# GNN weights in a PSUM bank, and the mix's softmax by eight biased, summing exponents

## The reference

```python
# GNN, one head: softmax over the edges that end in a node, times the rows of their sources
m = segment_max(e_h, dst); ex = exp(e_h - m[dst]); den = segment_sum(ex, dst)
out = segment_sum((ex / den[dst])[:, None] * z_h[src], dst)
# mix: softmax of q over the 32 features of each head
q = softmax(q, axis=-1) * SCALE
out = einsum('bhde,bhnd->bhne', context, q)
```

## Time and profile before

| | us |
|---|---|
| median of 3 runs | 2942.56 |
| lowest, highest | 2938.81, 2943.4 |
| the profiled execution | 2940.0 |
| its span, first to last instruction | 2937.9 |

### The profile page before, as it was taken

How to read it: one execution, slowest core, us unless ns; L and a number is a source line. 1 busy time by engine, 2 the same in 40 slices (tenths; PEclk the granted TensorE clock), 3 DMA queues, 4 the chain that set the end, 5 groups by cost and what they waited for, 6 DMA issues and landing times. The chain is left out here.

```text
span 2937.9 us, 21979 instructions
## 1 busy us (share of the span) xinstructions
PE 1496.6 (51%) x5476; PEld 949.3 (32%) x5476; DVE 2121.8 (72%) x3413; ACT 1206.4 (41%) x2381; POOL 2013.1 (69%) x1978
## 2 busy tenths in 40 slices
PE   2657730222212222222125179999899999984323
PEld 1433330111111111111025046555555555551122
DVE  6978889998888888888568255565655555657657
ACT  1532338776667776666334022222222232221012
POOL 0456457777777777777666677777777777777560
PEclk8878875555555555555555589999999999997666
DMA  4522547666666666666563312222222222222186
GB/s 137 186 68 68 148 126 238 229 225 214 209 204 216 219 218 207 218 218 213 190 176 105 107 30 49 49 67 51 49 49 49 49 53 53 61 50 44 17 304 230
DMA packets 222462, 395.96 MB, mean 135 GB/s; under 512 B 50867, under 2 KB 174370, under 8 KB 214912
## 3 DMA queue, kind: packets, MB, share of 16 engines
q1 hardware_dynamic: 137604, 263.49, 26.2%
q0 software_dynamic: 75632, 122.58, 18.0%
q10 hardware_dynamic: 9100, 8.50, 0.9%
HBM read 204.85 MB, written 189.59 MB: 134 GB/s over the span
## 5 line engine op out<-in xcount | busy, mean ns | idle before, releaser
L1234 POOL DMA_INDIRECT stage_got<-ffn_rows,setup_src_ffn x860 | 844.2, 982 | 261.8 <-issue 261.7
L1234 POOL DMA_INDIRECT edges_got<-gnn_rows,edges_src_gnn x728 | 756.4, 1039 | 241.7 <-issue 221.5
L1341 DVE TENSOR_TENSOR_SCAN stage_y<-stage_decays,stage_y 128x960 f32<-128x960 f32 (+2 forms) x256 | 520.7, 2088 | 5.1 <-issue 5.0
L2174 PE MATMUL stage_ph<-ffn_xt_all,stage_w 128*128 128x448 f32 x896 | 381.5, 566 | 102.0 <-ACT stage_hid L2235 40.3
L1357 ACT ACTIVATE stage_rows<-stage_y 128x3640 f32<-128x3640 f32 (+1 forms) x88 | 399.8, 4543 | 0.0
L1630 PE MATMUL stage_pm<-setup_ident,stage_mix_parts 128*128 128x128 f32 x98 | 33.4, 444 | 674.6 <-DVE stage_mix_parts L1703 602.3
L2296 DVE TENSOR_TENSOR stage_start_parts<-stage_pk,stage_of_tile 128x490 f32<-128x490 f32 x328 | 209.2, 667 | 115.8 <-PE stage_pk L2166 111.1
L2166 PE MATMUL stage_pk<-stage_start_parts 128*128 128x490 bf16 x984 | 244.3, 386 | 66.9 <-DVE stage_start_parts L2296 51.9
L1317 DVE TENSOR_TENSOR stage_y<-edges_got,stage_y 128x896 f32<-128x896 f32 x168 | 262.9, 1672 | 0.3 <-ACT stage_y L1299 0.3
L2174 PEld LDWEIGHTS stage_ph<-ffn_xt_all,stage_w 128*128 128x128 f32 x896 | 173.8, 197 | 243.9 <-issue 141.9
L1630 PEld LDWEIGHTS stage_pm<-setup_ident,stage_mix_parts 128*128 128x128 f32 x98 | 14.2, 204 | 705.0 <-DVE stage_mix_parts L1703 677.3
(11 more groups left out here) (481 smaller groups left out, 2903.3 us busy)
## 6 DMA issues: line engine op xcount, KB each, us to landing
state_gnn<-stage_rows SPq DMA_DIRECT2D x56, 1848.0 KB
y<-search_found SPq DMA_DIRECT2D x28, 896.0 KB, 4.2
tail_fin_y<-y SPq DMA_DIRECT2D x7, 3584.0 KB, 17.7
stage_got<-ffn_rows,setup_src_ffn POOLq DMA_INDIRECT x860
edges_got<-gnn_rows,edges_src_gnn POOLq DMA_INDIRECT x784, 3.6
state_ffn<-stage_rows SPq DMA_DIRECT2D x32, 384.0 KB, 2.4
mix_rows<-stage_mix_parts SPq DMA_DIRECT2D x49, 131.0 KB, 2.1
x_again_mix<-mix_rows SPq DMA_DIRECT2D x7, 917.0 KB, 6.1
```

Of the source, the lines that this page charges most:

```text
L1234: pool.indirect_dma_start(out=got[:, u, t, :], out_offset=None, in_=self.row_dram[g.name][:, :], in_offset=bass.IndirectOffsetOnAxis(ap=sr ...
L1341: ins = dve.tensor_tensor_scan(some, r[s][:, 0:b - a, :].rearrange("p c t -> p (c t)"), some, 0.0, ALU.mult, ALU.add)
L2174: mm = pe.matmul(ph[:, f % 2 * 2 + half, 0:HALF], w1[:, e, k, f * P:(f + 1) * P], xt_all[:, k, at(b * (B * P) + half * HALF, HALF)], start ...
```

## The change

The weights of the GNN get a PSUM bank of their own. ScalarE writes them there first (VectorE waits for that one), and a second time into `y`, where the scan and its own weighing want them; VectorE's three products read them from PSUM. In the mix the maximum is taken negated and kept for two tiles; ScalarE no longer exponentiates a shifted copy at once but reads `pq` directly, head by head, with that maximum as the bias, and accumulates each head's sum. Subtraction and sum on VectorE go; the maximum, the reciprocal and the product move to other places of the chunk; PE's next projection waits for the exponents.

```diff
+            weights = self.ps(stack, "weights", [P, 512])[:, 0:2 * H * T].rearrange("p (s h t) -> p s h t", s=2, h=H)
...
-                act.activation(y[:, s, C:C + H, 1:T + 1], pm[:, :, :], ACT.Exp).then_inc(w_ready, 1)
+                if g is GNN:
+                    act.activation(weights[:, s, :, :], pm[:, :, :], ACT.Exp).then_inc(w_ready, 1)
+                    act.activation(y[:, s, C:C + H, 1:T + 1], pm[:, :, :], ACT.Exp)
+                else:
+                    act.activation(y[:, s, C:C + H, 1:T + 1], pm[:, :, :], ACT.Exp).then_inc(w_ready, 1)
...
-                                            w[:, h, 0:n].unsqueeze(2).unsqueeze(3).to_broadcast([P, n, Q, KQ]), ALU.mult)
+                                            weights[:, s, h, 0:n].unsqueeze(2).unsqueeze(3).to_broadcast([P, n, Q, KQ]), ALU.mult)
...
-                        pe.wait_ge(q_shifted, t)
+                        pe.wait_ge(q_exp, t)
...
-                        act.wait_ge(q_shifted, t + 1)
-                        act.activation(q[:, 1 - s, :], q[:, 1 - s, :], ACT.Exp).then_inc(q_exp, 1)
+                        act.wait_ge(max_ready, t + 1)
+                        if t >= 2:
+                            act.wait_ge(q_turned, t - 1)
+                        for h in range(MIX_HEADS):
+                            d = at(h * MIX_DIM, MIX_DIM)
+                            ins = act.activation(q[:, 1 - s, d], pq[:, d], ACT.Exp, bias=mx[:, 1 - s, h:h + 1], scale=1.0,
+                                                 accum_out=sm[:, 1 - s, h:h + 1])
+                        ins.then_inc(q_exp, 1)
...
+                def q_max(t, s):
                     dve.wait_ge(projected, t + 1)
-                    dve.tensor_reduce(mx[:, :], by_head(pq[:, 0:D]), AX, ALU.max)
-
-                def q_shift(t, s):
-                    if not (isinstance(t, int) and t < 2):
-                        dve.wait_ge(q_turned, t - 1)
-                    dve.tensor_tensor(by_head(q[:, s, :]), by_head(pq[:, 0:D]), each(mx[:, :]), ALU.subtract).then_inc(q_shifted, 1)
-
-                def q_sum(t, s):
-                    dve.wait_ge(q_exp, t + 1)
-                    dve.tensor_reduce(sm[:, :], by_head(q[:, s, :]), AX, ALU.add)
+                    if t >= 2:
+                        dve.wait_ge(q_exp, t - 1)
+                    dve.tensor_reduce(mx[:, s, :], by_head(pq[:, 0:D]), AX, ALU.max, negate=True).then_inc(max_ready, 1)
...
                     edge.logits_sum(dve, c, b, u)
-                    if has(c, LAG + 1):
-                        q_sum(c - LAG - 1, s)
+                    if has(c, LAG):
+                        q_max(c - LAG, 1 - s)
                     dve.drain()
                     edge.logits_leaky(dve)
-                    if has(c, LAG + 1):
-                        q_share()
                     dve.drain()
                     edge.logits_max(dve, c, u)
                     if has(c, LAG + 1):
+                        q_share(c - LAG - 1, s)
+                    dve.drain()
+                    edge.logits_shift(dve, c, u)
+                    if has(c, LAG + 1):
                         q_norm(s)
-                    if has(c, LAG):
-                        q_max(c - LAG)
-                    dve.drain()
-                    edge.logits_shift(dve, c, u)
-                    if has(c, LAG):
-                        q_shift(c - LAG, 1 - s)
                     dve.drain()
                     edge.logits_out(dve, c, u)
```

More of the change, by code:

```diff
@@ L1541, in gnn_edges @@
                 [P, 2, D + 6],
-                [P, MIX_HEADS],
-                [P, MIX_HEADS])
+                [P, 2, MIX_HEADS],
+                [P, 2, MIX_HEADS])
             pq, pm = self.ps(here, "pq", [P, 512]), self.ps(here, "pm", [P, 512])
-            names = ("w_in", "ctx_turned", "ctxt_ready", "cw_made", "cw_ready", "projected", "q_shifted", "q_exp",
+            names = ("w_in", "ctx_turned", "ctxt_ready", "cw_made", "cw_ready", "projected", "max_ready", "q_exp",
                      "q_ready", "q_turned", "qt_ready", "mixed", "out_ready", "measured")
-            (w_in, ctx_turned, ctxt_ready, cw_made, cw_ready, projected, q_shifted, q_exp,
+            (w_in, ctx_turned, ctxt_ready, cw_made, cw_ready, projected, max_ready, q_exp,
              q_ready, q_turned, qt_ready, mixed, out_ready, measured) = (self.sem(here, n) for n in names)
@@ L1684, in _, with q_share @@
                 edge.dve_neg(dve)
-                def q_max(t):
+                def q_max(t, s):
                     dve.wait_ge(projected, t + 1)
-                    dve.tensor_reduce(mx[:, :], by_head(pq[:, 0:D]), AX, ALU.max)
-                def q_shift(t, s):
-                    if not (isinstance(t, int) and t < 2):
-                        dve.wait_ge(q_turned, t - 1)
-                    dve.tensor_tensor(by_head(q[:, s, :]), by_head(pq[:, 0:D]), each(mx[:, :]), ALU.subtract).then_inc(q_shifted, 1)
-                def q_sum(t, s):
+                    if t >= 2:
+                        dve.wait_ge(q_exp, t - 1)
+                    dve.tensor_reduce(mx[:, s, :], by_head(pq[:, 0:D]), AX, ALU.max, negate=True).then_inc(max_ready, 1)
+                def q_share(t, s):
                     dve.wait_ge(q_exp, t + 1)
-                    dve.tensor_reduce(sm[:, :], by_head(q[:, s, :]), AX, ALU.add)
-                def q_share():
-                    dve.reciprocal(sm[:, :], sm[:, :])
+                    dve.reciprocal(sm[:, s, :], sm[:, s, :])
                 def q_norm(s):
-                    dve.tensor_tensor(by_head(q[:, s, :]), by_head(q[:, s, :]), each(sm[:, :]), ALU.mult).then_inc(q_ready, 1)
+                    dve.tensor_tensor(by_head(q[:, s, :]), by_head(q[:, s, :]), each(sm[:, s, :]), ALU.mult).then_inc(q_ready, 1)
                 def measure(t, s, i):
@@ L1722, in step @@
                     if has(c, LAG + 1):
-                        q_norm(s)
-                    if has(c, LAG):
-                        q_max(c - LAG)
+                        q_share(c - LAG - 1, s)
                     dve.drain()
                     edge.logits_shift(dve, c, u)
-                    if has(c, LAG):
-                        q_shift(c - LAG, 1 - s)
+                    if has(c, LAG + 1):
+                        q_norm(s)
                     dve.drain()
@@ L1737, in _ @@
                 in_quads(step)
-                q_sum(NT - 1, 0)
-                dve.drain()
-                q_share()
+                q_share(NT - 1, 0)
                 dve.drain()
```

## The result

| | before | changed |
|---|---|---|
| median, us | 2939.25 (5 runs) | 2868.2 (5 runs) |
| lowest to highest | 2933.14 to 2943.4 | 2866.36 to 2870.12 |
| profiled execution | 2940.0 | 2866.36 |
| its span | 2937.9 | 2864.7 |

The ratio is 0.9757, 95% interval 0.9744 to 0.9771: 71 us faster. I had given 2877 with a range from 2868 to 2912; what was measured lies at its lower end, 2868.2 as a median and 2939.25 x 0.9757 = 2867.8 by the ratio. The direction and the mechanism held, and the gain came out larger than the 64 us of my sum.

The account below looks back on a forecast made before the run. GpSimd's issue of 14 gathers a chunk was taken as the bound. Terms of -65 (gathers), -1.2 (behind them) and +2 gave -64 from 2940.0, so 2876, given as 2877 us, range 2868 to 2912.

Parts of the forecast that it names:

- my sum: Whole kernel: -65 for gathers, -1.2 behind them, +2 for short products, together -64 us.
- The bound: Edge loop: GpSimd's issue of 14 gathers a chunk, 18.8 us, sets the pace although VectorE is busier.
- rival D: Edge loop: the transfers bind, DMA share 0.64 becoming 0.69; about half the gain lost, 2905 us; chance 0.04.
- The gathers' term: Gathers beside the weighing: 3 a chunk return to 0.947 us, -65; +2 reserved for short two-SBUF products meeting gathers.
- The gather of 2.78 us: Later stage: a gather beside a scan with both inputs in SBUF, cited as evidence that two SBUF inputs hold gathers.
- rival (C): Weighing: its scattered writes, not the second SBUF input, stretch the gathers; time stays 2938 to 2941 us; chance 0.07.
- The bounds of 1.08 and 2.0: Lower and upper limits in us for one weighing product of 896 elements with PSUM weights; no change taken.
- VectorE's edits: Mix: subtraction and sum go, -0.83 us a chunk; worth nothing inside the loop, -1.2 us behind the last gather.
- ScalarE's edits: Weights and mix: one more weights exponent, eight summing exponents for one; 3.2 us a chunk, covered, costed at nothing.
- x: Time of one 32-element summing exponent on ScalarE: taken 0.40 us, upper bound 0.56; ScalarE becomes the bound from 0.59.
- the slow rival (B): ScalarE becomes the bound: 2880 to 2935 us, chance 0.06; slower than before, such as 2999 us, 0.06.
- The two readings of the hold: Skill on VectorE and GpSimd: two-SBUF instructions block gathers, whole term; or tensor_tensor spares descriptor generation, term zero.

Follow-up runs that it names:

- the second comparison: The changed kernel unaltered beside the kernel before on one chip, 9 runs: 2871.18 against 2938.86 us, ratio 0.9768.
- the two loads beyond it: Changed kernel with two more weighing-shaped products on VectorE: 2965.58 us; changed kernel with ScalarE's eight summing exponents made three times: 2987.48 us.

## Why the mechanism held, and where the sum was off

**The step that failed.** It is the sum: its two terms, -65 + 2 for the gathers and -1.2 behind them, were both taken too small. Between the first and the last gather -63 was forecast and -66.4 measured; behind them -1.2 was forecast and -1.7 measured. That makes 68 us instead of 64, which the second comparison finds too. Two things more lie between 2877 and 2868.2. The forecast went out from a median of before of 2942.56, and the five runs of the comparison give 2939.25, 3.3 us of the difference. And 3 of the first comparison's 71 us lie outside the loop and are not found again: scatter, as far as the traces tell. I had the lower end of the range made from my terms' ends (70 us) off the lowest run of before, and it left no room for that scatter: the lowest of all runs of before is 2930.78 and the highest 2948.59.

**The bound.** Right. GpSimd's issue set the pace before and sets it after; VectorE's idle time for gathers fell from 101.3 to 64.4 us, as VectorE's work shrank less than GpSimd's time. Extra work on either engine that stayed within GpSimd's 17.5 us a chunk cost 10 to 12 us in the loop, of 84 and 103 added; the two loads beyond it cost 92 and 119. The transfers didn't bind (rival D): the DMA engines' share rose to 0.69 as forecast, and the median landing fell from 3.6 to 3.3 us.

**The gathers' term, -65 and +2.** The mechanism was right: a product with one SBUF and one PSUM input holds no gather, and one with two holds each gather that starts beside it, to its end. All of the stretching went, and the reserve of +2 us for short products that would meet a gather in every chunk was not needed: gathers over 1.0 us away from the weighings are 13 in the trace of before, with 1.8 us of stretching, and 8 in that of after, with 1.4. They stand beside the mix's product, which has two SBUF inputs.

One row behind the mechanism was misread. The gather of 2.78 us ends at 1703.77, 1.6 us after the scan beside it and 0.12 us after the cast that follows the scan. So the scan alone didn't hold it that long; whether the cast did, no run isolates. The first scan of the same three shows the hold by itself, in the trace of before:

```profile
1695.36 2.33 DVE L1019 TENSOR_TENSOR_SCAN edges_ffn_ed_edge<-stage_start_parts 128x1024 f32<-128x1024 f32 x1
1696.50 1.94 POOL L1234 DMA_INDIRECT stage_got<-ffn_rows,setup_src_ffn  x1 [0.30 <-issue]
...
1702.29 1.36 DVE L2271 CAST stage_start_parts<-stage_by_node 128x980 bf16<-128x980 f32 x1
```

The scan ends at 1697.69 and the gather at 1698.44, 0.75 us after it. So a contiguous scan with two SBUF inputs holds a gather as well, to 1.94 us and not to 2.78; the argument against rival (C) stands.

**The weighing.** No change was forecast and none came, 1.667 against 1.672 us. The bounds of 1.08 and 2.0 were not touched; the lower one was drawn from contiguous products, and no form tried came near it.

**VectorE's edits.** Right inside the loop: nothing. Behind it, 1.2 us were forecast for them, and they have less: 46.2 us became 45.5 with the mix's edits alone, 45.2 with the weights alone and 44.5 with both. About 0.7 to 1.0 us belong to each; the weights' part wasn't in the sum.

**ScalarE's edits.** One exponent with its read-out costs 0.26 us from start to start, not 0.40: 2.1 us a chunk instead of 3.2. The read of the accumulator overlaps the exponent ahead of it. The exponents start 0.75 us late, I had said 1.0, and the carry is not late at all. But the room was overrated: I put the threshold at x = 0.59, and with the ring through PE of 0.84 us a chunk, left out of my sum, it is lower: (17.5 - 12.8 - 0.84) / 8 = 0.48. My own upper bound of 0.56 would have been beyond it, so the slow rival (B) deserved more than the 0.12 that it got. The exponents made three times show it: that is x = 0.79, for which my sum gives 79 us over the changed kernel, and 119 were measured, slower than the kernel before.

**The two readings of the hold.** In every kernel run, a gather that starts beside a weighing's product with two SBUF inputs ends 0.7 to 0.8 us after that product, and takes up to 2.5 us; one beside a product with a PSUM input takes 0.95 us. The Trainium skill, "SBUF — State Buffer", section "Who interferes with whom", has both readings: that such an instruction blocks a GpSimd one that reads SBUF, and, as an inference, that tensor_tensor leaves descriptor generation alone. By the first, the term was the whole of the stretching, by the second nothing; the measurement decides for the first.

## What to carry to other kernels

Find the engine that never waits, even if another is busier: here GpSimd at 69% of the span set the pace, and its instructions' spread (0.947 us in the median, 1.039 in the mean) was the gain. Then ask what runs beside the long ones: a VectorE product or scan that reads two tiles from SBUF held each gather that started beside it to its end, and one input moved to a PSUM bank, for one short instruction of ScalarE, freed it. Count a hold by phase, which is how much of the instruction is left when the gather starts, and not by the number of instructions. When the room of an engine is estimated, add its rings through other engines, since they are idle time that it can't fill. And where work runs behind the bound's last item, an engine that only just keeps pace pays there for what it is behind.

## What the runs showed of the hardware

- A single product of 1.67 us with two SBUF inputs held gathers for 48 us over 56 chunks, three in a row for 65: the gathers fall into step behind the first, and the two that follow lose 0.27 us each.
- A gather that starts 0.05 us ahead of such a product is not held (0.95 us), one that starts 0.03 us behind its start is (2.37 us). A held gather ends 0.70 to 0.73 us after the product in the same kernel, whatever the length of the hold.
- Up to five products in a row with one SBUF and one PSUM input leave a gather at 0.946 us in the mean.
- An exponent of 32 numbers with a bias pointer and an accumulated sum is two instructions on ScalarE, 0.17 and 0.09 us from start to start.
- The same 896 products take 1.67 us with scattered writes and 1.78 us with scattered reads, whether the weights come from PSUM or SBUF in the first case.
